# Delta ahead of B and C before the first state, and products of constants in TensorE's waits

## The reference

```
x = x + 0.5 * ffn(norm(x))       # 256 -> 1024 -> 256, weights of -1, 0, 1, gelu
x = x + attention(norm(x))       # causal, 16 heads of 16, rope
x = x + 0.5 * ffn(norm(x))       # the same ffn
x = x + 0.5 * moe(norm(x))       # shared swiglu + 2 of 16 experts per token
x = x + mamba(norm(x))           # below
x = x + 0.5 * moe(norm(x))       # the same moe
```

```
x_, z   = in_proj(norm(x))                       # 512 + 512 channels
x_conv  = silu(causal 4-tap convolution of x_)
dt_low, B, C = x_proj(x_conv)                    # 128, 16, 16
delta   = softplus(dt_proj(dt_low) + bias)       # 512 channels
h_t     = exp(delta_t * A) * h_(t-1) + delta_t * B_t * x_conv_t   # 16 states per channel
y_t     = sum over the 16 states of h_t * C_t;  y = (y + D * x_conv) * silu(z)
out_proj(y)
```

## Time and profile before

| | us |
|---|---|
| three runs | 920.31, 920.41, 914.29 (median 920.31) |
| the profiled execution | 914.37 |
| its span, first to last instruction | 913.1 |
| mean granted TensorE clock | 0.879 |

### The profile page before, as it was taken

One profiled execution on the slowest core, in us unless ns is written; L12 is line 12 of the kernel. 1 busy time (PEld: TensorE's weight loads), 2 busy tenths in 40 slices (PEclk: granted clock), 3 DMA queues, 4 the chain that ended last, 5 costly groups with the idle time before them and its releaser, 6 DMA issues. The chain is left out here.

```text
span 913.1 us, 11010 instructions
## 1 busy us (share of the span) xinstructions
PE 698.9 (77%) x3650; PEld 473.5 (52%) x3650; DVE 591.6 (65%) x1014; ACT 372.6 (41%) x754; POOL 346.4 (38%) x422
## 2 busy tenths in 40 slices
PE   3978897889886886599278478879788878676990
PEld 2766453444333674488256345545445545445880
DVE  6877544776632777344386787788987798862333
ACT  3421333254674332033133944586554444221330
POOL 3223222111112302536410155666656667234462
PEclk9998778778998797899679679999999999978995
DMA  4945722020000901355400000000051000013435
GB/s 177 297 61 88 95 37 38 2 36 2 1 1 12 426 21 47 135 177 172 150 1 0 1 0 1 1 1 1 1 203 74 0 1 1 34 36 129 130 120 179
DMA packets 37496, 65.96 MB, mean 72 GB/s; under 512 B 11474, under 2 KB 27474, under 8 KB 35810
## 3 DMA queue, kind: packets, MB, share of 16 engines
q1 hardware_dynamic: 32930, 52.87, 20.5%
q0 software_dynamic: 4512, 12.39, 3.8%
HBM read 39.63 MB, written 21.69 MB: 67 GB/s over the span
## 5 line engine op out<-in xcount | busy, mean ns | idle before, releaser
L1265 PE MATMUL PS<-FB,C 128*128 128x512 f32 x256 | 134.1, 620 | 3.8 <-DVE FB L1926 3.8
L1365 ACT ACTIVATE FA<-PS 128x512 f32<-128x512 f32 (+3 forms) x192 | 80.1, 504 | 68.6 <-PE PS L1035 68.3
L2057 POOL TENSOR_TENSOR FB<-FB,RBF 128x512 f32<-128x512 f32 x51 | 65.8, 1290 | 82.9 <-DVE FB L1917 82.9
L2003 POOL TENSOR_SCALAR_AFFINE_SELECT FA<-FA 128x128 f32<-128x128 f32 x128 | 36.3, 295 | 125.7 <-ACT FA L1365 123.4
L494 PE MATMUL PS<-C,FB 128*128 128x128 f32 x250 | 44.0, 297 | 48.9 <-DVE FB L1579 27.2
L2038 POOL DMA_INDIRECT GY<-FB x62 | 61.0, 984 | 52.1 <-DVE FB L1813 21.1
L1647 DVE TENSOR_REDUCE FA<-PS 128x2 f32<-128x1024 f32 (+2 forms) x64 | 67.9, 1085 | 18.8 <-PE PS L1014 18.5
L494 PEld LDWEIGHTS PS<-C,FB 128*128 128x128 f32 x250 | 34.2, 152 | 60.5 <-DVE FB L1579 27.8
L1035 PE MATMUL PS<-RA 64*128 64x512 f32 (+3 forms) x192 | 57.7, 467 | 5.2 <-ACT FA L1365 5.1
L1797 DVE TENSOR_TENSOR FB<-FB,PS 128x256 f32<-128x256 f32 (+1 forms) x32 | 13.2, 413 | 74.4 <-ACT FB L1403 74.4
L1158 PE MATMUL PS<-WE,FB 128*128 x248 | 61.2, 390 | 0.0
(11 more groups left out here) (273 smaller groups left out, 1575.5 us busy)
## 6 DMA issues: line engine op xcount, KB each, us to landing
WE<-in_wr SPq DMA_DIRECT2D x8, 1536.0 KB, 11.4
FB<-GX SPq DMA_DIRECT2D x14, 520.0 KB, 3.8
RA<-RA SPq DMA_DIRECT2D x48, 128.0 KB, 4.8
FB<-GY SPq DMA_DIRECT2D x8, 512.0 KB, 5.6
GX<-GX SPq DMA_DIRECT2D x1, 4030.0 KB, 27.7
GX<-FA SPq DMA_DIRECT2D x1, 3968.0 KB, 16.4
FA<-in_w SPq DMA_DIRECT2D x2, 1024.0 KB, 7.2
FA<-in_qkvo SPq DMA_DIRECT2D x1, 1536.0 KB, 20.0
```

The lines of the kernel that those rows point to most:

```text
L1265: pe.matmul(bank(m), ident, shc[k % 4], start=n == 0, stop=n == DN - 1).then_inc(*yad.inc(ch, n, m))
L1365: act.activation(PT[n % 12][:, c0:], bank(ring_bank[(x, *a)])[:, c0:], ACT.Exp, scale=0.25).then_inc(*exd.inc(*a))
L2057: pool.tensor_tensor(shc[k % 4], sh[k % 5], Cs[(stc.no[ch, n] - 1) % 2], ALU.mult).then_inc(*cma.inc(ch, n, m))
```

## The change

Two things.

1. **Products of constants.** A helper `busy(out, n)` issues n bf16 matmuls of 128x128 ones and a constant triangle, 512 columns each, into a bank of PSUM that is free at that moment; nothing reads the result. It is called ahead of waits of PE:

| ahead of | n |
|---|---|
| `tr` (2,0), (3,1), (4,0), (5,1) | 16, 5, 20, 7; (4,0) first waits for the first `yload`, (5,1) for the last add of the mamba block |
| `up` (1,0,0) | 6 |
| `oproj` (1,0) | 7 |
| `route` (u,1), both u; `route` (0,0) | 6; 8, behind its wait for `xadd` |
| `rank` u, both | 7 |
| `sgu` (u,1,0), both | 8 |
| `e1` (u,0), both | 26; the wait for the shared expert's add now stands behind them and ahead of that for `fetch` |
| `in` (0,0) | 6, behind its wait for the last expert pair |
| `dt` (0,0) | 6 |
| `trb` (0) | 10 |
| `tru` (0,1), (0,2), (0,3) | 3 each |

2. **The order before the first state.** `dt` and `dta` of all four groups come directly behind `xdt` and `dts`; `in` (1,5) to (1,7) and `xbc` (B and C) follow; the silus of z for chunk 1 are a step of their own (`inz`), three of the four behind `dtl`. Tap 0 of chunk 1's convolution moves from DVE to ACT, `dut` of chunk 0 from ACT to DVE, `dg` (0,0) from ACT to POOL. `silu` (1,·) stands behind `dtl`.

The diff, cut to its core:

```diff
+IDLE_TURN = {(2, 0): 16, (3, 1): 5, (4, 0): 20, (5, 1): 7}
...
-    yield [("xdt", 0, v) for v in range(3)] + conv(1, 0, 0) + [("xbc", 0, v) for v in range(3)] + [("dts", 0)] + conv(1, 0, 1)
...
+    yield conv(1, 0, 0) + conv(1, 1, 0) + [("xdt", 0, v) for v in range(3)] + [("dts", 0)] + proj(1, 4) + [("inz", 4)] + conv(1, 0, 1)
     for m in range(4):
-        yield [("du", 0, m), ("tru", 0, m), ("dut", 0, m)]
+        yield [("dt", 0, m), ("dta", 0, m)]
+    yield proj(1, 5, 6, 7) + conv(1, 0, 2) + [("dte", 0, m) for m in range(4)] + conv(1, 0, 3)
+    yield [("xbc", 0, v) for v in range(3)] + conv(1, 1, 1, 2, 3) + [("dtl", 0), ("bct", 0), ("trb", 0), ("spB", 0, 1), ("spC", 0, 0)]
+    yield [("inz", m) for m in (5, 6, 7)] + [("du", 0, 0), ("tru", 0, 0), ("du", 0, 1), ("btx", 0), ("tru", 0, 1), ("stB", 0, 1), ("stC", 0, 0), ("dg", 0, 0)]
+    yield [("silu", 1, 0), ("silu", 1, 1), ("du", 0, 2), ("dut", 0, 0), ("tru", 0, 2), ("du", 0, 3), ("dut", 0, 1), ("tru", 0, 3), ("dut", 0, 2), ("dut", 0, 3)]
...
+            def busy(out, n):
+                for _ in range(n):
+                    pe.matmul(out, TRI[:, P:2 * P], TRI[:, 0:P].unsqueeze(1).broadcast_to([P, 4, P]), start=True, stop=True)
...
+                    if (s, ch) in IDLE_TURN:
+                        if (s, ch) == (4, 0):
+                            pe.wait_ge(*yld[0].at(0, 0))
+                        elif s == 5:
+                            pe.wait_ge(*mlx.at(TC - 1))
+                        busy(out[0], IDLE_TURN[s, ch])
...
                     bk = bank(4 * (pi % 2))
+                    if pi == 0:
+                        busy(bk, 26)
+                        pe.wait_ge(*sad.at(u))
                     if pi % 2 == 0:
                         pe.wait_ge(*fet[gi % 2].at(u, gi))
-                    if pi == 0:
-                        pe.wait_ge(*sad.at(u))
...
+                elif x == "conv" and a[0] == 1 and a[2] == 0:
+                    act.wait_ge(*pre.at(1))
+                    for m in (2 * a[1], 2 * a[1] + 1):
+                        act.wait_ge(*ine.at(1, m))
+                        act.activation(xc[1][:, m, :], xrs[1][:, m, 0:512], ACT.Identity, scale=cw[:, 4 * m:4 * m + 1]).then_inc(*cv0.inc(m))
...
+                elif x == "dut" and a[0] == 0:
+                    _, i = a
+                    dve.wait_ge(*tru.at(0, i))
+                    dve.tensor_copy(DUT0[:, :, i * P:i * P + P], bank7("tru", 0, i).rearrange("p (t n) -> p t n", t=TC)).then_inc(*dud.inc("turned", i))
...
+                elif x == "dg" and a == [0, 0]:
+                    pool.wait_ge(*btd.at(0))
+                    for i in range(TC):
+                        t = pool.tensor_scalar(diag[0][:, i * P:i * P + P], ident, BT[0][:, i, 0:1], None, ALU.mult)
+                    t.then_inc(*bmd.inc("diag"))
```

More of the change, by code:

```diff
@@ L599, in build @@
         pre = sig("s_conv_pad", [(ch,) for ch in range(NCH)])
+        cv0 = sig("s_conv_first", [(m,) for m in range(4)])
         cvd = sig("s_conv", [(ch, 2 * h + v) for ch, h in of("silu") for v in range(2)])
@@ L608, in build @@
         dln = sig("s_dt_ln", of("dtl", 0, 1, 2, 3))
-        dud = sig("s_du", of("du"))
+        dud = sig("s_du", [(x[1:] if x[0] == "du" else ("turned", x[2])) for x in plan if x[0] == "du" or x[:2] == ("dut", 0)])
         spb, stb = sig("s_bspread", of("spB")), sig("s_bstore", of("stB"))
         trb, btc, btd = sig("s_b_tr", of("trb")), sig("s_b_copy", of("btx")), sig("s_b_turned", of("btx"))
-        tru, dut = sig("s_du_tr", of("tru")), sig("s_du_turned", of("dut"))
-        dgd = sig("s_diag", of("dg"))
+        tru, dut = sig("s_du_tr", of("tru")), sig("s_du_turned", [k for k in of("dut") if k[0]])
+        dgd = sig("s_diag", of("dg")[1:])
         spc, stc = sig("s_cspread_even", of("spC")), sig("s_cstore", of("stC"))
@@ L952, in tensor_program @@
                     if f == 0:
+                        if u == 1 and ch == 0:
+                            busy(bank(4), 6)
                         pe.wait_ge(*xno.at(2 * u, ch, 1))
@@ L1072, in tensor_program @@
                     if i == 0:
+                        if ch:
+                            busy(bk, 7)
                         pe.wait_ge(*atl.at(ch))
@@ L1080, in tensor_program @@
                         pe.wait_ge(*xad.at(1, 1))
+                    if ch:
+                        busy(bank(ch), 6)
+                    elif u == 0:
+                        busy(bank(ch), 8)
                     pe.wait_ge(*xno.at(s, ch, 1))
@@ L1090, in tensor_program @@
                     u, = a
+                    bk = bank(2)
+                    busy(bk, 7)
                     pe.wait_ge(*hotd.at(u))
-                    bk = bank(2)
                     for t in range(NT):
@@ L1105, in tensor_program @@
                     else:
+                        if ch == 0:
+                            busy(bank(4), 8)
                         pe.wait_ge(*smd.at(u, n - 1, ch))
@@ L1182, in tensor_program @@
                     if m == 0:
+                        if ch == 0:
+                            pe.wait_ge(*e4e[1].at(0, len(PAIRS) - 1 - len(PAIRS) % 2))
+                            busy(bank(0), 6)
                         pe.wait_ge(*xno.at(4, ch, 1))
@@ L1207, in tensor_program @@
                     if m == 0:
+                        if ch == 0:
+                            busy(bk, 6)
                         pe.wait_ge(*dtl.at(ch))
@@ L1212, in tensor_program @@
                     bk = claim7(x, ch)
+                    if ch == 0:
+                        busy(bk, 10)
                     pe.wait_ge(*bcl.at(ch))
@@ L1220, in tensor_program @@
                     if ch == 0:
+                        if i:
+                            busy(bk, 3)
                         pe.wait_ge(*dud.at(0, i))
@@ L1236, in tensor_program @@
                     if ch == 0 and n == 1:
-                        pe.wait_ge(*dut.at(0, TC - 1))
+                        pe.wait_ge(*dud.at("turned", TC - 1))
                     if n > 1:
@@ L1300, in emptied @@
             assert plan.index((out, *key)) < plan.index(here if here in plan else here + (0,))
-            pe.wait_ge(*(drl.at(key[1]) if name == "dt" and key[0] == 0 else done.at(*key)))
+            if key[0] == 0 and name == "dt":
+                pe.wait_ge(*drl.at(key[1]))
+            elif key[0] == 0 and name == "tru":
+                pe.wait_ge(*dud.at("turned", key[1]))
+            else:
+                pe.wait_ge(*done.at(*key))
         def wait7(*here):
@@ L1450, in scalar_program @@
                     act.activation(BTh, bank7("trb", ch).rearrange("p (t n) -> p t n", t=TC)[:, :, 0:64], ACT.Copy).then_inc(*btc.inc(ch))
-                elif x == "dut":
+                elif x == "dut" and a[0] == 1:
                     ch, i = a
                     act.wait_ge(*tru.at(ch, i))
-                    to = DUT0[:, :, i * P:i * P + P] if ch == 0 else DUT[ch][i]
-                    from_ = bank7("tru", ch, i)
-                    act.activation(to, from_ if ch else from_.rearrange("p (t n) -> p t n", t=TC), ACT.Copy).then_inc(*dut.inc(ch, i))
+                    act.activation(DUT[ch][i], bank7("tru", ch, i), ACT.Copy).then_inc(*dut.inc(ch, i))
                 elif x == "dte":
```

29 lines of the change are left out of this document (13 added, 16 removed).

## The result

The changed kernel took **908.35 us** (median of 4 runs, 903.75 to 912.26), beside 917.33 for the kernel before (4 runs, 914.29 to 920.41): ratio 0.9867, 95% interval 0.9819 to 0.9914. The forecast was 898 in a range of 886 to 911. The sign and the range held; of the 19 us of gain forecast, 9 came. The two medians alone give 0.990, inside that interval: a ratio here is not the quotient of the medians beside it. In a later sitting the ratio was 0.9886 [0.9826, 0.9947]. Executions in the slower state that this chip sometimes shows are left out of every ratio and median here.

A forecast was written before the change was run, and what follows sets the result against it. A chain of stages in which engines wait for each other, with PE's clock at half after waits. Products 11.2, order 7.1 and state 0.7 sum to 19.0 us: 895.4 from the profile, 901.3 from the median, middle 898; range 886 to 911.

The forecast's parts named there:

- the clock does not answer: Rival: in most places products are few and end too early; the order alone gives, 911 us; chance 0.11.
- Second ffn: Products at `oproj` (1,0) gain 1.0 us; those at `tr` (2,0) and `up` (1,0,0) together 2.4, bounds 0 and 3.
- First moe's front: Products before the first moe's experts: `route` (0,1) gains 1.2 us, `rank` 0.6, `route` (0,0) delays 0.6; net 1.3.
- `e1`: 26 products ahead of the first experts in both moes: about 35% that the clock holds, 0.8 and 0.65 us; bounds 0 and 4.1.
- `tr` (4,0) and `in`: Products ahead of the mamba projection: 12 matmuls of `in` run at 0.22 instead of 0.43, 2.5 us gained, bounds -0.8 and 2.6.
- Second moe's front: Products before the second moe's experts: transposes 0.8 us, `route` (1,1) 1.2, `rank` 0.6; together 2.6, bounds -1 and 3.
- The order: From `dts` to the first scan: new order gains 6.0 us, full clock at `bringC` and `pb` 1.1; 7.1, bounds 3 and 9.
- First units of the state: Start of the state stage: PE at full clock in place of half gives 0.7 us, bounds 0 and 2.
- The first rival: Transposes do not hold the clock, so stretches alternating products and transposes stay partly at half: 901 us, chance 0.12.
- the order gives nothing: Rival before the first scan: DVE, with four copies more, is late, or the scans wait for `bm` anyway: 905 us, chance 0.12.
- more: Rival: both `e1` start at full clock and the state too: 892 us, chance 0.08.
- Slower: Rival: products run at half clock and outlast their waits, 21 us or so against the order's 5 to 7: 935 us, chance 0.05.

The follow-up runs named there:

- again: The changed kernel once more, unedited, in a later sitting beside the kernel before: 911.65 us, ratio 0.9886.
- best: Changed kernel without products at `e1`, `rank`, `route` (0,0); new ones at both ends of the state stage and 4 at each of eight attention waits: 899.12 us, 0.9755.

## Why the prediction was right in sign and range, and 10 us too low

The forecast 895.4 for the profiled execution was 13.6 us under the 908.98 that it took. Of these, 4.8 are the attention, 0.3 lie outside the span, and 8.5 are terms of the sum (the products gave 6.0 of the 11.2 us, the order 6.4 of 7.1, and the state and `mol` took back 2.1; 0.3 came in the last stage). That the time still fell in the range is in part luck: 911 was set by the rival in which the clock does not answer, and that is not what happened.

- **Second ffn** (`oproj` 1.0, `tr` and `up` 2.4): right, 3.15 measured by stage, 2.9 by taking them out. The share was other than I put it: all of it was there by the first gelu, as PE was at full clock from `oproj` on; the ups and downs behind it gained nothing more, the ffn being 37.1 to 37.2 long in before, after, again and best.
- **First moe's front**, 1.3: it gave 0.7. `route` (0,1) as computed. `rank` was guessed at half of 1.34 and took 1.26, so its 0.6 was not there, in either moe: its matmuls start 27 ns apart at half clock and 25 at full. That weight loads set this pace, as I wrote, is not shown. The delay of `route` (0,0) was put at 0.6; without its products and those of `rank` the stage is 0.8 shorter.
- **`e1`**, 1.45: the step that failed most. It gave -2.2 (66.1 and 66.0 for 65.2 and 64.7). The chance that the clock holds, 35%, was generous: it fell in both moes within the 3.9 us left. And the bound "0" at the lower end was wrong, for two reasons. With the products the clock fell only 0.7 and 0.9 us ahead of `e1` instead of 5.6 and 3.3, and it came back 1.5 and 2.4 us later behind the start of `e1`; at half speed that costs 0.8 and 1.2 us, and PE's work in these stages is 0.8 and 1.2 longer, nearly all of the 0.9 and 1.3. And I took the room for a fixed number of the kernel; in the later executions VectorE's last step of the shared expert starts 5 to 8 us later, counted from the one-hot, and the products are in the way.
- **`tr` (4,0) and `in`**, 2.5: right, 2.5.
- **Second moe's front**, 2.6: 1.8 (the missing `rank`, 0.6, and 0.2).
- **The order**, 7.1: 6.4, and its chain right to 0.3 us at the last ln and the last turned copy. What was missing is the clock at `pb`: of the 1.1 us for a full clock, 0.9 were not there, as PE waits 1.14 us ahead of `bringC`, in a place without products. In other executions `pb` was at full clock and the stage took 24.4, so the step moves by 1 us from one execution to another.
- **First units of the state**, 0.7: not there; the first nine scans take 19.8 us before and after, and the whole stage is 0.4 longer. In six of the twelve profiles of the new order the nine take 18.6, so this term too depends on the execution.
- **Not in the sum**: `mol`, +1.7. With the new order the clock falls in PE's last waits of the state stage, in seven of the eight profiles that have no products there. I had asked where the clock was half in the kernel before, and not where it was only just held.

The rule of the Trainium skill that I weighed ("TensorE: Matmul & The Clock Gate", Part 1: under 1% for the ramp) gave, as an estimate, at most 9.1 us for the products, I took 11.2. The products alone measured 0.66% [0.27, 1.05], so the page's figure was the better of the two. But the products of the best version give more than that figure: 0.9755 against 0.997 for the order alone is 2.2%, across two sittings. The first rival, that stretches where products and transposes alternate stay at half, fell: the clock was 1.00 in 504 to 511, and was lost only behind the last transposes. The statement beside it (Part 4 of that page, transposes do not open the clock) is not touched by that, since the products stood between the transposes.

Of the other rivals, "the order gives nothing" is refuted by the stages (7.1 us to the first scan with the order alone), though in the time the order alone is not clear of 1; "the clock does not answer" is refuted, and "more" did not come, as both `e1` started at half. "Slower" had half of the mechanism, products that outlast their wait, which 44 products do, and 26 in part; but they do it at full clock, since the wait shrank, and not because they ran at half. Its 935 is also 2 us more than its own terms give from the middle of 917.3 (21.5 less 6).

## What to carry to other kernels

A product that keeps the clock pays where it ends shortly ahead of the wait's end and the work behind it is bound by matmul columns (`oproj`, `route`, `in`, `mol`), not where idle time is left behind it (`e1`, where half clock then lasted longer than without the products) or where the work is many small matmuls (`rank`, 16 columns each). Size it by the shortest room that several executions show, since one profile's room can be gone in the next: here 44 instead of 26 turned a gain of 1.3% into nothing. And compare two profiles stage by stage before you explain their difference, so that a stage that nobody touched is seen to move.

## What the runs showed that I had not expected

- In the attention, the same instructions end at 286.9 to 296.5 us in thirteen profiles, later where the clock granted is lower (0.85, 0.82, 0.80 in the rows above). It is not all of the spread: of the two profiles of the changed kernel, the one with the earlier end of the attention (288.9 against 292.5) has the longer span (911.3 against 907.4), for the hold in the moes.
- A wait of 7 to 10 us on VectorE, behind one of ScalarE, with no releaser in the profile, in both moes of every profile of three sittings and in neither of the first two.
- Four multiplications of 128x128 by GpSimd took 3.10 us (L2091), as many elements as one 128x512, which takes it 1.50 (L2102).
